# Loading edge rows and name halves at a round's second scatter landing instead of its last

## The reference

```python
h = relu(layernorm(x))
x = x + (segment_sum(h[src], dst) / max(deg, 1)) @ W_l.T + h @ W_r.T     # layer 0
h = relu(layernorm(x))
agg = segment_sum(edge_attr, src, num_segments=N)                         # layer 1
z = concat([h, agg]) @ W1 + b1
z = batchnorm(silu(z));  z = batchnorm(silu(z @ W2 + b2))
x = x + z @ W3 + b3
```

## Time and profile before

| | us |
|---|---|
| median of 3 runs | 1402.36 |
| lowest and highest | 1400.37, 1403.76 |
| the profiled execution's own time | 1403.72 |
| span of its trace | 1402.0 |
| TensorE's mean granted clock, share of full | 0.92 |
| stage B's scatters in that trace | 645.3 to 1062 |

### The profile page before, as it was taken

How to read it: one execution, slowest core, us unless ns; L and a number is a source line. 1 busy time by engine, 2 the same in 40 slices (tenths; PEclk the granted TensorE clock), 3 DMA queues, 4 the chain that set the end, 5 groups by cost and what they waited for, 6 DMA issues and landing times.

```text
span 1402.0 us, 22062 instructions
## 1 busy us (share of the span) xinstructions
PE 1014.0 (72%) x5275; PEld 732.3 (52%) x5275; DVE 1072.2 (76%) x4647; ACT 876.0 (62%) x1708; POOL 879.6 (63%) x625
## 2 busy tenths in 40 slices
PE   0227677677776666766988888898976667999776
PEld 0125555555554444544655656565654553447765
DVE  2428888888877667666999899998963887788966
ACT  1227677677765565552877777786874876669610
POOL 7778788888888888876777777877761000002443
PEclk9969999999999998897999999998987878999999
DMA  9988888877776666667899999999989983216999
GB/s 331 371 298 198 221 209 211 215 171 159 172 159 137 139 154 136 135 146 185 204 240 234 239 233 223 263 220 240 228 241 289 352 276 122 90 60 237 418 418 362
DMA packets 184284, 313.25 MB, mean 223 GB/s; under 512 B 21840, under 2 KB 73462, under 8 KB 184194
## 3 DMA queue, kind: packets, MB, share of 16 engines
q1 hardware_dynamic: 116026, 264.44, 54.3%
q0 software_dynamic: 62720, 38.57, 23.2%
q10 hardware_dynamic: 5448, 9.29, 1.8%
HBM read 162.44 MB, written 149.79 MB: 223 GB/s over the span
## 4 chain that ended last, share of the span: by engine, by line
POOL 43%; DMA 22%; issue 17%; PE 11%; DVE 4%; ACT 1%; SPq 0%; DVEq 0%; POOLq 0%; ACTq 0%
POOL acc L916 22%; POOL acc L936 10%; DMA acc<-zT,worn 8%; POOL xin L894 7%; PE ps L1777 6%; DMA acc<-tabs,worn 5%; POOL zT L902 4%; DMA zT<-x_dram 4%; PE ps L1748 2%; DMA xin<-acc 2%; DMA res<-acc 1%; PE ps L1787 1%; DMA acc<-zT,tabs 1%; DVE zT L1598 1%; DVE zT L1602 1%
## 5 line engine op out<-in xcount | busy, mean ns | idle before, releaser
L1646 PE MATMUL ps<-zT 128*128 128x512 f32 (+5 forms) x784 | 272.7, 499 | 135.5 <-ACT zT L1055 128.0
L916 POOL DMA_INDIRECT acc<-zT,tabs x196 | 317.4, 1619 | 68.4 <-issue 62.0
L1646 PEld LDWEIGHTS ps<-zT 128*128 128x128 f32 (+1 forms) x784 | 165.3, 217 | 264.3 <-issue 134.9
L1381 DVE BATCH_NORM_STATS2 zT<-zT 128x6 f32<-128x128 f32 (+1 forms) x384 | 78.9, 278 | 170.8 <-DMA zT<-in_x_dram 170.8
L936 POOL DMA_INDIRECT acc<-zT,worn x100 | 156.6, 1566 | 53.5 <-issue 26.2
L936 POOL DMA_INDIRECT acc<-tabs,worn x96 | 150.2, 1565 | 52.2 <-issue 25.1
L894 POOL DMA_INDIRECT xin<-in_x_dram,tabs x140 | 141.3, 1009 | 42.6 <-issue 42.1
L1015 ACT ACTIVATE hT<-ps 128x1024 f32<-128x1024 f32 (+1 forms) x100 | 100.1, 1003 | 65.7 <-PE ps L1638 53.1
L1656 PE MATMUL ps<-weights_ab,zT 128*128 128x128 f32 (+1 forms) x784 | 126.4, 286 | 5.7 <-ACT zT L1022 5.3
L1638 PE MATMUL ps<-ident,zT 128*128 128x128 f32 (+1 forms) x784 | 118.9, 301 | 8.2 <-ACT zT L1007 7.6
L1290 DVE SCALAR_TENSOR_TENSOR zT<-ps,worn,zT 128x128 f32<-128x128 f32 (+1 forms) x196 | 95.2, 541 | 37.4 <-PE ps L1691 37.1
(11 more groups left out here) (194 smaller groups left out, 2145.9 us busy)
## 6 DMA issues: line engine op xcount, KB each, us to landing
acc<-bst SPq DMA_DIRECT2D x12, 2112.0 KB, 20.4
acc<-bst SPq DMA_DIRECT2D x48, 528.0 KB
zT<-in_x_dram SPq DMA_DIRECT2D x48, 512.0 KB, 6.5
zT<-acc SPq DMA_DIRECT2D x48, 512.0 KB, 4.8
zT<-x_dram SPq DMA_DIRECT2D x42, 512.0 KB, 10.0
out_dram<-zT SPq DMA_DIRECT2D x42, 512.0 KB, 10.2
zT<-row_dram SPq DMA_DIRECT2D x49, 256.0 KB, 5.7
zT<-in_edge_attr_dram SPq DMA_DIRECT2D x48, 256.0 KB
```

Of the source, the lines that this page charges most:

```text
L916: pool.indirect_dma_start(acc1, bass.IndirectOffsetOnAxis(ap=target_a[:, k, j:j + 1], axis=0), v[:, j, :], None, compute_op=ALU.add).then_ ...
L1646: ins = nc.tensor.matmul(psA[:, 0:j + 1, 0:p], t[0:p, j, :], same[0:p, par, at:at + j + 1, 0:p], start=(j == ROWS - 1), stop=(j == 0))
```

## The change

The call of `load_b_edges` in `step_b` moves from behind the wait for the fourth landing and the load of acc rows to just behind the wait for the second landing, ahead of the y load and the x1 store. The argument `held`, which made the tail's load wait for the fourth landing, is gone.

```diff
-            def load_b_edges(i, par, tail, spill, held=False):
+            def load_b_edges(i, par, tail, spill):
...
-                if held:
-                    sp.wait_ge(*two_ago(s_end2, par, i - 1, 16))
...
                 sp.wait_ge(*this(s_sc2, par, i, 32))
                 if not before and ahead:
                     load_b_nodes(*ahead)
+                if 2 * (i + 2) + par <= RF:
+                    load_b_edges(i + 2, par, i + 2 == IT, 0)
                 if third and third[3]:
...
                 if third:
                     sp.wait_ge(*this(s_end2, par, i, 16))
                     load_b_nodes(*third)
-                if type(i) is not int or 2 * (i + 2) + par <= RF:
-                    load_b_edges(i + 2, par, type(i) is int and i + 2 == IT, 0, held=True)
```

## The result

The changed kernel took 1427.45 us (median of 6 runs, 1424.26 to 1431.23), the kernel before 1401.36 us on the same chip (6 runs, 1393.82 to 1404.6). The ratio is 1.0196, with a 95% interval of 1.0171 to 1.022. The change makes the kernel 26 us slower. The forecast was 1394.4 us in a range of 1384 to 1406: wrong in sign, and out of the range.

The account below looks back on a forecast made before the run. Stage B was taken as bound by how fast each round's second scatter lands; 11.3 us gained less 3.0 us lost, taken as 8, from 1403.72 gives 1395.7, less 1.4 to the median: 1394.4 us, range 1384 to 1406.

Parts of the forecast that it names:

- What bounds B: Stage B, rounds 6 to 45: second landings set the time; GpSimd waits 30.8 us for landings, 0.77 us a round.
- By so much the backlog that the next second scatter has to sit out is shorter: After second landings in stage B: the moved load fills idle DMA time, at most 0.76 us a step; 11.3 us in 40 rounds.
- The halves ... I cost this at nothing: Stage B: early halves end TensorE's 41.5 us and VectorE's 22.6 us of waits, worth nothing since GpSimd never waits for VectorE.
- The y step's cost: Every third step, which also loads y: late fourth landings delay third scatters, 0.76 us in four such steps, 3.0 us back.
- The rule against the change: DMA engines take turns between queues, so a scatter would not care about SyncE's backlog length; 0 in place of 8 us.
- Slower: Rival, chance 0.19: the moved load delays fourth landings in the 13 y steps, costing 8.6 us; 1411 us.
- No change: Rival, chance 0.22: a scatter's landing depends on whether there is a backlog, not on its length; 1402.4 us.
- 1: Sign: TensorE's wait for halves falls from 41.5 us to under 10, and VectorE's 22.6 with it.
- 2: Sign: GpSimd's idle time in stage B falls by some 8 us, only before first scatters.
- 3: Sign: the DMA share between second landing and accumulator load rises.
- 4: Sign: in y steps, waits appear before third scatters, a few tenths of a us each.
- 5: Sign: the stages before and behind stage B keep their times to 1 us.

Follow-up runs that it names:

- e2: The kernel before with only the 256 KB of edge rows loaded at the second landing, the halves staying late; 1412.62 us.
- e10: The kernel before with edge rows early only in steps that also load y, the halves staying late; ratio 1.0036.
- e1: The kernel before with only the 2 KB of halves loaded at the second landing, the edge rows staying late; 1421.42 us.
- e5: The kernel before with only the halves loaded early and stage B's z stores cut from 512 KB to 64 KB; 1405.03 us.
- e4: The kernel before with stage B's z stores cut from 512 KB to 64 KB; 1399.06 us.
- e15: The changed kernel with z and x1 stores of y steps held until GpSimd has processed the next round's second scatter; 1405.84 us, ratio 1.0027.
- e11: The changed kernel with the z store of y steps held until GpSimd has processed the next round's second scatter; 1425.08 us, ratio 1.0165.
- e14: The changed kernel with the x1 store of y steps held until GpSimd has processed the next round's second scatter; ratio 1.0165.
- e3: The changed kernel with stage B's z stores cut from 512 KB to 64 KB; 1416.89 us.

## Why the prediction was wrong

- **What bounds B: right.** Second landings set the time. 24.6 of the 25 us in the 40 rounds are waits of GpSimd for landings, and its work and pauses stay as they were to 1.2 us.
- **"By so much the backlog that the next second scatter has to sit out is shorter": this step failed.** It supposed that the edge rows were in that scatter's way already. In y steps they were not: step 17 issued them at 802.13, 3.2 us behind the landing, and by the mean of y steps at 4.35 us, when that scatter's record ends (4.37); in 7 of the 12 y steps of rounds 7 to 43 they were issued behind that end. The move put 256 KB in front of it that had mostly stood beside or behind it. e2 and e10 show that alone: 8.6 us, and 4 to 5 us where it is done in y steps only. I had the numbers for this in the earlier trace rows and asked only what the load would fill where it went, not what it had filled where it stood: the time around the next second landing. The windows of steps 16 to 20 above show that hole.
- **"The halves ... I cost this at nothing": this step failed, and it was the larger.** That they would be in time for VectorE was right. That GpSimd doesn't wait for VectorE was right as well, and beside the point: ScalarE, released with VectorE, issues the z store, and GpSimd waits for what that store delays. The z store doesn't occur in the prediction at all. e1 (17.4 us), e5 (the same with a small z store, 0.3% over e4) show it.
- **The y step's cost: wrong in sign.** I expected the fourth landing to slip and third scatters to wait. It comes earlier in the mean of y steps, 1.67 us behind the second landing instead of 3.24, probably since the fourth scatter now finds the DMA engines emptier. That is part of the damage: the accumulator load, issued at that landing, is now in front of the next second scatter as well.
- **The rule against the change.** The prediction weighed the Trainium skill's sentence (DMA: Bandwidth & Descriptors, "Queues, rings and completion order") that an engine takes turns between queues. By it, landing would not depend on the length of the other queue's backlog. The y steps here don't bear that out. From the end of the second scatter's record to its landing it takes 3.8 us in the mean where 1280 KB were issued between the second landing and that end (25 rounds of the changed kernel) and 6.3 us where 2304 KB were (12 rounds). And from 809.6 to 813.5 us q0 got no turn beside q1's 655 packets; it did beside transfers that were issued behind the scatter (e15). The measurement decides: the backlog ahead counts. Its bytes alone don't give the time, though: with 1792 KB it takes 6.0 us in e11 and e14, 4.9 in e2 and 4.7 in the kernel before. My own test at the end ("then backlog length is not what holds a scatter") would have led to the wrong conclusion: landings became longer with the halves in time, because the backlog was longer.
- **The rivals.** "Slower" had the right sign and the wrong place. It went through the fourth landing in y steps; the loss goes through the second one, at three times the price. "No change" had landings that don't depend on the backlog's length, and they do.
- **What should show it.** 1: half. VectorE's wait went; TensorE's for the halves stayed at 36.0 us: all 27 of these waits now end 1.3 to 1.9 us behind a second landing, at which the halves are issued. 2: reversed, + 25.8 us, though the places (first scatters) were right. 3: reversed, from 0.79 to 0.50 between second landing and accumulator load (rounds 7 to 43). 4: didn't occur. 5: B's start holds to 0.3 us, the rest is 3.2 us shorter.

**Open.** Why one 512 KB store held takes at most 0.3 us off the y step and two take 2.5. With 1792 KB in front the y step is 10.4 us in e11 and e14, but 8.9 and 9.2 in e2 and e10, whose z store goes out 6 us or more behind the landing. e3 and e11 differ by 448 KB of z issued right behind the second scatter, and by 1.0 us of y step. So with 1792 KB in front it seems that what comes close behind counts too; with 1280 KB in front (e15) 1024 KB behind do not. No run here varied the amount finely enough to say where that turns.

## What to carry to other kernels

Ask of a transfer that is moved forward what it did in its old place: issuing everything at one event puts it all in front of the scatter that is waited for next, and here left the DMA engines emptier at its landing. When a load is made early, list every DMA that the released engines issue and find where those land; a 2 KB load moved 512 KB here. Count the bytes that stand between a landing and the scatter that is waited for next, by kind of round; the mean over rounds hides the one in three that pays.

## What was not expected of the hardware

- An increment behind an indirect DMA on GpSimd is carried out before that DMA has started (785.48 against 786.57 us); a memset behind it is not: its record ends 0.1 us behind the scatter's end. The mark's record lasts 0.70 us, but 0.57 us of it lie under the scatter, and the next scatter starts 1.86 us after the last as without it (801.56, 803.42). 17 of them cost nothing that can be measured.
- The scatters' queue moved no packet while SyncE's queue worked off what had been issued ahead (809.6 to 813.5 us after the change, 0 beside 655), but moved beside what was issued behind it (e15, 288 beside 349).
- The bytes in front of the second scatter don't give the y step's length by themselves: 8.15 us with 1280 KB (e15), but 8.9 (e2) to 10.4 (e11) with 1792.
